# Multiplying the gate into tanh plus one ahead of the value product, and the odd slot's tanh ahead of the second pair of blocks

## What is computed

```python
h = layernorm(x) * (1 + ca) + sa
x = x + ga * attn(h)            # projections, 2048-step recurrence, C and D products
h = layernorm(x) * (1 + cb) + sb
xr = mu_r * h + (1 - mu_r) * h_prev      # h_prev: the token before
xk = mu_k * h + (1 - mu_k) * h_prev
r = sigmoid(xr @ W_r.T)
k_act = square(relu(xk @ W_k.T))
x = x + gb * (r * (k_act @ W_v.T))
```

## Time and profile before

| | us |
|---|---|
| median of 3 executions (lowest to highest) | 1007.74 (1007.02 to 1007.92) |
| the profiled execution | 1007.41 |
| its span, first to last instruction | 1004.8 |
| TensorE busy | 945.0 (94%) |
| VectorE busy | 777.4 (77%) |
| ScalarE busy | 766.8 (76%) |
| GpSimd busy | 120.8 (12%) |
| TensorE in the chain that ended last | 76% of the span |

### The profile page before, as it was taken

One profiled execution on the slowest core, in us unless ns is written; L12 is line 12 of the kernel. 1 busy time (PEld: TensorE's weight loads), 2 busy tenths in 40 slices (PEclk: granted clock), 3 DMA queues, 4 the chain that ended last, 5 costly groups with the idle time before them and its releaser, 6 DMA issues.

```text
span 1004.8 us, 14776 instructions
## 1 busy us (share of the span) xinstructions
PE 945.0 (94%) x4992; PEld 784.2 (78%) x4992; DVE 777.4 (77%) x2137; ACT 766.8 (76%) x1599; POOL 120.8 (12%) x123
## 2 busy tenths in 40 slices
PE   4746999999999999999999999999999999999997
PEld 1325887888888888888888887888888888887886
DVE  0586979787878978796887978797897878797653
ACT  6768887889878787987878788887878798745541
POOL 1250011110201011010101011020101002000000
PEclk9879899999999999999999999999999999999999
DMA  7650112021211302121120302112120211111001
GB/s 246 230 188 0 65 42 75 10 84 43 73 65 43 95 17 68 43 84 44 43 95 29 104 7 84 42 53 74 43 95 6 97 35 42 43 43 43 22 22 42
DMA packets 35259, 64.77 MB, mean 64 GB/s; under 512 B 3688, under 2 KB 4328, under 8 KB 35184
## 3 DMA queue, kind: packets, MB, share of 16 engines
q1 hardware_dynamic: 35184, 63.84, 18.9%
HBM read 47.02 MB, written 16.81 MB: 64 GB/s over the span
## 4 chain that ended last, share of the span: by engine, by line
PE 76%; ACT 10%; DVE 8%; issue 2%; DMA 2%; POOL 1%; SPq 1%; DVEq 0%; ACTq 0%
PE ps_kr L302 32%; PE ps_cd L302 18%; PE ps_tv L302 13%; PE ps_pt L302 8%; PE ps_tv L344 2%; PE ps_pt L310 2%; DVE mix_full L812 2%; ACT square_out L497 1%; ACT mix_full L596 1%; DVE tmp L1013 1%; ACT rt L633 1%; ACT mix_r_hi L607 1%; ACT L633 1%; ACT h_full L525 1%; DMA mix_full<-in_w_b 1%
## 5 line engine op out<-in xcount | busy, mean ns | idle before, releaser
L812 DVE SCALAR_TENSOR_TENSOR mix_full<-ps_tv,cur_m,mix_full 128x256 f32<-128x256 f32 x256 | 121.4, 478 | 60.4 <-ACT mix_full L596 60.4
L1200 POOL TENSOR_SCALAR var<-sq 128x2 f32<-128x2 f32 (+1 forms) x48 | 29.7, 618 | 810.1 <-ACT square_out L497 810.1
L596 ACT ACTIVATE mix_full<-ps_tv,cur_m 128x255 f32<-128x255 f32 x256 | 119.9, 574 | 0.2 <-PE ps_tv L344 0.2
L615 ACT ACTIVATE kk<-ps_kr 128x512 f32<-128x512 f32 x64 | 36.5, 589 | 108.8 <-PE ps_kr L302 108.8
L302 PE MATMUL ps_kr<-mix_k_hi,wk_hi 128*128 128x256 f32 x512 | 82.4, 283 | 3.0 <-ACT rt L633 2.6
L514 ACT ACTIVATE x_in<-x_in,norm_bias,rstd 128x512 f32<-128x512 f32 x64 | 47.0, 805 | 46.8 <-POOL norm_bias L1207 46.8
L302 PE MATMUL ps_kr<-mix_k_hi,wk_lo 128*128 128x256 f32 x512 | 81.2, 280 | 0.0
L302 PE MATMUL ps_kr<-mix_k_lo,wk_hi 128*128 128x256 f32 x512 | 81.1, 280 | 0.0
L302 PEld LDWEIGHTS ps_kr<-mix_k_hi,wk_hi 128*128 128x128 f32 x512 | 70.8, 189 | 10.2 <-issue 8.5
L302 PE MATMUL ps_tv<-wv_hi,kk_hi 128*128 128x512 f32 x256 | 71.1, 399 | 5.6 <-issue 5.6
L302 PE MATMUL ps_kr<-wr_hi,mix_r_hi 128*128 128x512 f32 x256 | 71.4, 400 | 0.8 <-ACT kk L615 0.8
(11 more groups left out here) (172 smaller groups left out, 2292.9 us busy)
## 6 DMA issues: line engine op xcount, KB each, us to landing
x_in<-in_x SPq DMA_DIRECT2D x16, 1024.0 KB, 5.2
x<-in_x SPq DMA_DIRECT2D x32, 512.0 KB, 3.7
out<-x SPq DMA_DIRECT2D x32, 512.0 KB, 2.7
x<-in_wmod SPq DMA_DIRECT2D x4, 1024.0 KB, 6.4
mix_full<-in_wmod SPq DMA_DIRECT2D x2, 1024.0 KB, 7.4
x<-in_wd SPq DMA_DIRECT2D x1, 1024.0 KB, 5.0
x<-in_wr SPq DMA_DIRECT2D x1, 1024.0 KB, 7.3
x<-in_wv SPq DMA_DIRECT2D x1, 1024.0 KB, 5.5
```

Source lines behind the costliest of these rows:

```text
L596: mm = act.activation(mix[n][:, k, 1:UNIT], ps_tv[:, j, c * UNIT:(c + 1) * UNIT - 1], ACT.Identity, bias=cur_m[:, SHIFT + k:SHIFT + k + 1] ...
L615: act.activation(kk[:, i, :], ps_kr[:, i, :], ACT.Relu).then_inc(s_relu, 1)
L812: dve.scalar_tensor_tensor(mix[n][:, k, :], ps_tv[:, j, c * UNIT:(c + 1) * UNIT], cur_m[:, alpha + k:alpha + k + 1], mix[n][:, k, :], ALU. ...
L1200: pool.tensor_scalar(var[:, :], sq[:, :], 1.0 / D, EPS, ALU.mult, ALU.add).then_inc(s_var, 1)
```

## The change

VectorE's `read_out` no longer adds one to tanh. A new generator `gated_tanh` forms (tanh + 1) x `gate_b` in place as soon as tanh is there, two instructions a unit; `read_out` multiplies that with the value product; `add_out` adds the result to x. The number of VectorE instructions for the tail of a unit stays six. `gated_tanh(u)` stands in its own slot: in an even one behind two steps of the recurrence and ahead of `residual(u + 2)`, in an odd one between `normalise2(u + 2)` and `h_low` of the second pair, with one recurrence step beside each instruction. The place of the former gate products is empty, and the recurrence steps dealt out beside them are taken later. On ScalarE the odd slot's tanh, with its table load, moves ahead of the second pair of blocks.

```diff
@@ block.scalar, odd slot
                     if next_mix:
                         mix_high(u + 1, 1)
+                    tanh(u)
                     if next_t1:
                         h_blocks(q + 3, (2, 3))
                         h_high(q + 3, (2, 3))
-                    tanh(u)
@@ block.vector
-            def read_out(u):
-                for i in range(TPU):
-                    dve.wait_ge(s_v, u * TPU + i + 1)
-                    dve.wait_ge(s_rt, u * TPU + TPU + i + 1)
-                    dve.scalar_tensor_tensor(rt[:, i, :], rt[:, i, :], 1.0, ps_tv[:, i, :], ALU.add, ALU.mult)\
-                       .then_inc(s_rv, 1)
-                    yield
-            def gated_out(u):
+            def gated_tanh(u):
                 if u % UPB == 0:
                     dve.wait_ge(s_gate_b, u // UPB * 16 + 16)
                 for i in range(TPU):
+                    dve.wait_ge(s_rt, u * TPU + TPU + i + 1)
+                    dve.scalar_tensor_tensor(rt[:, i, :], rt[:, i, :], 1.0, gate_b[:, :], ALU.add, ALU.mult)\
+                       .then_inc(s_rvg, 1)
+                    yield
+            def read_out(u):
+                for i in range(TPU):
+                    dve.wait_ge(s_v, u * TPU + i + 1)
+                    dve.wait_ge(s_rvg, u * TPU + i + 1)
+                    dve.tensor_tensor(rt[:, i, :], ps_tv[:, i, :], rt[:, i, :], ALU.mult).then_inc(s_rv, 1)
+                    yield
+            def add_out(u):
+                for i in range(TPU):
                     dve.wait_ge(s_rv, u * TPU + TPU + i + 1)
-                    dve.tensor_tensor(rt[:, i, :], rt[:, i, :], gate_b[:, :], ALU.mult).then_inc(s_rvg, 1)
-                    yield
-                for i in range(TPU):
-                    dve.wait_ge(s_rvg, u * TPU + i + 1)
                     dve.tensor_tensor(x2[:, u % 4, i, :], x2[:, u % 4, i, :], rt[:, i, :], ALU.add).then_inc(s_out, 1)
                     yield
...
                 if u % 2 == 0:
                     if u:
                         beside(rec, read_out(u - 1), 2)
-                        beside(rec, gated_out(u - 1), 2)
+                        beside(rec, add_out(u - 1), 2)
...
                         run(mix_low(u + 1, 1))
                     take(rec, 2)
+                    run(gated_tanh(u))
                     if next_cd:
                         run(residual(u + 2))
...
                 else:
-                    beside(rec, gated_out(u - 1), 2)
+                    beside(rec, add_out(u - 1), 2)
...
                         beside(rec, normalise2(u + 2), 1)
+                    beside(rec, gated_tanh(u), 1)
                     if next_t1:
                         beside(rec, h_low(q + 3, (2, 3)), 1)
             run(read_out(NUNIT - 1))
-            run(gated_out(NUNIT - 1))
+            run(add_out(NUNIT - 1))
```

More of the change, by code:

```diff
@@ L841, in normalise2 @@
                     yield
+            def gated_tanh(u):
+                if u % UPB == 0:
+                    dve.wait_ge(s_gate_b, u // UPB * 16 + 16)
+                for i in range(TPU):
[3 more added lines that the diff above has]
+                    yield
             def read_out(u):
@@ L846, in read_out @@
                     dve.wait_ge(s_v, u * TPU + i + 1)
-                    dve.wait_ge(s_rt, u * TPU + TPU + i + 1)
-                    dve.scalar_tensor_tensor(rt[:, i, :], rt[:, i, :], 1.0, ps_tv[:, i, :], ALU.add, ALU.mult)\
-                       .then_inc(s_rv, 1)
+                    dve.wait_ge(s_rvg, u * TPU + i + 1)
+                    dve.tensor_tensor(rt[:, i, :], ps_tv[:, i, :], rt[:, i, :], ALU.mult).then_inc(s_rv, 1)
                     yield
-            def gated_out(u):
-                if u % UPB == 0:
-                    dve.wait_ge(s_gate_b, u // UPB * 16 + 16)
+            def add_out(u):
                 for i in range(TPU):
                     dve.wait_ge(s_rv, u * TPU + TPU + i + 1)
-                    dve.tensor_tensor(rt[:, i, :], rt[:, i, :], gate_b[:, :], ALU.mult).then_inc(s_rvg, 1)
-                    yield
-                for i in range(TPU):
-                    dve.wait_ge(s_rvg, u * TPU + i + 1)
                     dve.tensor_tensor(x2[:, u % 4, i, :], x2[:, u % 4, i, :], rt[:, i, :], ALU.add).then_inc(s_out, 1)
```

## The result

| | before | after |
|---|---|---|
| median of 4 executions each (lowest to highest), us | 1007.83 (1007.02 to 1008.64) | 1024.23 (1022.54 to 1027.83) |
| ratio to before, 95% interval | | 1.0163 (1.0144 to 1.0182) |
| profiled execution: time, span | 1007.41, 1004.8 | 1027.83, 1025.1 |

What follows compares the result with a forecast made beforehand. Bound: TensorE, released in odd slots by `kk_lo` on a chain without slack. Before 1007.41, 13 pairs at +1.39 (+18.1), unit 28 +1.1, tail -1.2: 1025.4 profiled, 1025.7 us median; range 1014 to 1034.

Steps and rivals of the forecast that it cites:

- The bound: In the loop TensorE is always busy; `kk_lo` releases the odd slot's value product, on a chain without slack.
- Even slot, +1.20: Two gate products behind `om_pos` delay the residual, and through it the odd slot's `mix_full`, by 1.20 us.
- Odd slot, +0.75: Wider recurrence steps beside the odd slot's mixes lengthen VectorE's path from `mix_full` to `kk_lo` by 0.75 us.
- Tanh, -0.56: With the odd slot's tanh earlier, the K product follows `kk_lo` after 5.75 instead of 6.31 us: -0.56.
- (e): The forecast itself holds: 1.1 to 1.75 us a pair, 1022 to 1030 us in all; 60%.
- (d): More than counted: recurrence ends past the evictions (1039 us at one microsecond) or stalls lower TensorE's clock (1030); 12%.
- End of the recurrence: Ends later in even slots, hidden with 1.2 us left; in unit 28 exposed, costing +1.1 us.
- Tail, -1.2: After the loop, the last two gate products are done while the last value product runs: -1.2 us.
- The stalls: Sign: value product stalls in 13 odd slots, 1.5 us or 2.3 to 3.1 each, 24 to 30 in all.
- (a): The pairs' delays are absorbed, waits for tanh and the tail's 1.2 us go: 1004 us; 6%.
- (b): Only one of the pair's two delays counts: 1016 us if steps are free, 1010 if products are; 15%.
- (c): GpSimd gets quicker as gate products leave its side, saving 1.0 us in each of 7 pairs: 1019 us; 7%.

Runs made afterwards that it cites:

- experiment 1: Kernel before plus two unread 128x512 VectorE products of two SBUF operands where the changed kernel's even-slot gate products stand; 1027.96 us, ratio 1.0186.
- experiment 2: Changed kernel with the even slot's two gate products ahead of the two recurrence steps (`om_pos`) instead of behind them; 1006.40 us, ratio 0.9974.
- experiment 5: Changed kernel with four recurrence steps instead of two beside each addition to x in odd slots; 1014.14 us, ratio 1.0052.
- experiment 6: Changed kernel with the four recurrence steps at the start of odd slots all ahead of the two additions to x; 1009.50 us, ratio 1.0016.
- experiment 7: Kernel before with eight recurrence steps at the start of odd slots ahead of the gate products and additions; 999.38 us, ratio 0.9910.
- experiment 8: Changed kernel with the rest of the recurrence run ahead of the mixes in unit 28 alone; 1020.62 us, ratio 1.0117.

## Why the prediction was right, point by point

**The bound.** Right. That the release of the value product is `kk_lo`, 0.10 ahead of it, holds in all 13 odd slots of the changed kernel, and experiment 1 shows that the chain from the even slot's residual has no room.

**Work.** Right: VectorE is busy 778.8 us instead of 777.4.

**Even slot, +1.20.** The mechanism is shown twice: put in, it costs 1.3 (experiment 1), moved two instructions up, 1.20 come back (experiment 2). The term was mis-sized all the same, as a sum for the slot. From the K product to the new x it grew by 0.80 in slot 4, because something else in the slot got 0.41 shorter: before, the mixes of the even slot were held up too by wide recurrence steps, which I looked for in the odd slot only. ScalarE before, slot 4:

```profile
234.25 0.63 ACT L607 ACTIVATE mix_k_hi<-mix_full 128x512 fp32r<-128x512 f32 x1 [0.41 <-DVE mix_full L812]
```

In the changed kernel this wait is gone, in 12 of the 13 pairs (0.41 in nine of them, 0.7 in three; unit 0 had none). Experiment 5 shows the reverse: with the steps put back beside the odd additions, the wait is back in these 12, the even slot is longer by 0.83, and the odd path shorter by 0.82. Over the 13 pairs the way to the new x grew by 8.5 us, where 13 x 1.20 = 15.6 were forecast. Of the 7.1 between them the waits are 5.8; the rest wasn't followed up.

**Odd slot, +0.75.** Measured 0.72 in slot 5 (`kk_lo` is 1.52 later after its pair's K product, of which 0.80 had come with relu), 9.7 in the 13 pairs for 9.75 forecast.

**Tanh, -0.56.** From `kk_lo`'s end to the K product it was 6.31 before and is 285.65 - 279.88 = 5.77 now: -0.54. Units 4 to 6 together: 0.80 + 0.72 - 0.54 = 0.98, and their distance grew by 0.98. Pairs that were longer before grew by less (units 24 to 26, 58.29 before, by 0.53). All 13, without the falls: 8.5 + 9.7 - 6.8 = 11.4, a mean of 0.87, for 18.1 forecast. So the term that was mis-sized is the even slot's; a mean of 0.87 also lies below the 1.1 to 1.75 a pair of (e).

**The clock.** The forecast had no term for it; rival (d) named it, with "a fall for 3 us behind the three longest would add some 4.5". It was 3 x 1.55 = 4.65, and it hid most of what the pairs had been overrated by. That the total of the pairs came to 16.0 where 18.1 had been forecast is therefore partly luck: of the two errors, -6.7 in the mechanism and +4.65 in the clock, most cancel. Without the three falls the median would be some 1019.6 (an estimate, 1024.23 - 4.65): still slower by 1.2%, but outside the 1022 to 1030 of (e).

**End of the recurrence.** In the even slots hidden, as forecast, but with the cover used up. In slot 6 the state ends 303.24 - 285.65 = 17.59 after the K product (before 14.24), 3.35 later where 2.9 were forecast, and ScalarE takes it up 0.13 after that:

```profile
302.81 0.43 DVE L1039 TENSOR_TENSOR state<-tmp,f 128x256 f32<-128x256 f32 x1
```

```profile
303.37 0.42 ACT L574 ACTIVATE xs<-state 64x256 f32<-64x256 f32 x1
```

The forecast of 1.2 us left was wrong; 0.1 is left, since `xs` itself also begins earlier after the K product (303.37 - 285.65 = 17.72, before 297.33 - 279.00 = 18.33). In unit 28 the stall is 3.74 for 3.4 forecast, so +1.4 where +1.1 was said, and 2.3 more in an execution in which the clock falls behind it.

**Tail, -1.2.** Measured -1.22.

**The stalls.** 24 to 30 us were forecast; the 13 odd slots have 19.3, 0.75 to 2.96 in each. Where a stall stood before it is now 1.75 to 2.96 (2.3 to 3.1 forecast), where none stood 0.75 to 1.03 (1.5 forecast): they are short mostly by what the even slot gave back, 7.1 in all. In the slots without a stall the room for `kk_lo` had also been 0.22 to 0.41, not a quarter of a microsecond everywhere.

**The rivals.** (a) and (b) are out: both delays were seen. (c) ended as no part of this change, but the reading against it was wrong. I took the rule of the Trainium skill as not borne out, since "VectorE's order at that place is the same in both slots". It isn't: slot 6's kind has the short copy L771 ahead of the first gate product, and slot 4's has not. And both kinds get shorter once the products leave (experiments 6 and 7). GpSimd did not get quicker in the changed kernel because the additions, with two SBUF operands like the gate products, moved up into exactly their places. The right question would have been what stands beside GpSimd afterwards, not what leaves.

## What to carry to other kernels

Work that fills an engine's time belongs ahead of the instruction that waits, not behind it: two products behind a wait of 1.26 us cost 18 us more than the same two ahead of it, and there the whole of VectorE's part costs 1.2 us (1006.40 against the 1005.18 of tanh alone). Where steps are dealt out between the instructions of a chain, moving one instruction changes which steps stand beside every later link, so look at all links, and at what takes an emptied place. Where a small GpSimd operation is on the chain, compare its duration between places and runs, and try the wide VectorE instructions with two SBUF operands elsewhere. And a stall of some 2 us can bring another 1.5 us through TensorE's clock.

## What the runs showed of the hardware

In seven of the 13 pairs GpSimd's power on 128x4 elements takes 3.27, 2.66 or 2.06 us with two, one or no 128x512 VectorE instruction of two SBUF operands between its start and the second 256-column step, and ends 0.4 after that step in every profile. In the other six it takes 1.41 whatever stands beside it, and the norm bias behind it 1.07, 0.47 or 0.33. Moving the products behind the steps was worth 8 us to the kernel before, by order alone.

TensorE's clock fell to 0.50 behind some stalls and not behind others of the same length: it fell behind 2.96, 2.09 and 1.83 us in the changed kernel (both profiles, the same three pairs) but not behind 1.85 in the pair of unit 24; not behind 2.08 and 1.83 without the tanh move; in the first pair behind 2.07 in experiment 2 and not behind 2.06 in experiment 5; in experiment 1 behind 2.02 in unit 25 and not behind 2.00 in units 9 and 17; and behind 3.7 in unit 28 in one profile and not in the other. So the length of the stall alone doesn't decide, and what does is open.

Open too: whether the copy L771 makes the 1.0 us by which GpSimd's part of the chain differs from pair to pair (power 3.27 against 1.41 before), at which moments GpSimd can be held up, and why the stretch ahead of the loop varies by 2.7 us between profiles. The granted clock of the first 100 us varies with it in part: 0.86 in experiments 5, 6 and 8, which enter the loop at 104.9 to 105.3, and 0.88 to 0.90 in the others, at 102.5 to 104.9.
